# Another order for VectorE's operations inside each step of a graph-attention kernel's edge loop

## The reference, cut to what matters

```python
kj = k[src] + e                     # e = edge features @ We
alpha = sum(q[dst] * kj, axis=-1) / sqrt(C)
m = segment_max(alpha, dst)
a = exp(alpha - m[dst])
s = segment_sum(a, dst)
vj = v[src] + e
out = segment_sum((a / s[dst])[..., None] * vj, dst)
```

## Time and profile before

| what | value |
|---|---|
| median of the runs | 7153.44 us |
| the profiled execution, its own time | 7176.55 us |
| its span, first to last instruction | 7174.9 us |
| POOL busy | 5053.5 us, 70% |
| VectorE busy | 4453.4 us, 62% |
| TensorE busy | 4422.2 us, 62% |
| ScalarE busy | 997.8 us, 14% |
| moved over the span | 94 GB/s on average |

### The profile page before, as it was taken

One profiled execution on the slowest core, in us unless ns is written; L12 is line 12 of the kernel. 1 busy time (PEld: TensorE's weight loads), 2 busy tenths in 40 slices (PEclk: granted clock), 3 DMA queues, 4 the chain that ended last, 5 costly groups with the idle time before them and its releaser, 6 DMA issues. The chain is left out here.

```text
span 7174.9 us, 154717 instructions
## 1 busy us (share of the span) xinstructions
PE 4422.2 (62%) x36620; PEld 3475.0 (48%) x36620; DVE 4453.4 (62%) x15728; ACT 997.8 (14%) x4122; POOL 5053.5 (70%) x5118
## 2 busy tenths in 40 slices
PE   7996555555555556665656565566555555555555
PEld 5775444444444445444444444445444444444444
DVE  6556666666666666666666666666666666666666
ACT  2222111111111112111111111112111111111110
POOL 2225777777777775777777777775777777777775
PEclk8995555555555555555555555555555555555555
DMA  4553333333333333333333333333333333333332
GB/s 121 159 154 95 89 90 91 90 90 90 90 91 91 90 90 88 93 92 91 92 90 94 91 92 91 92 93 89 92 89 89 90 90 90 90 91 90 90 89 71
DMA packets 687687, 675.84 MB, mean 94 GB/s; under 512 B 369234, under 2 KB 506388, under 8 KB 687636
## 3 DMA queue, kind: packets, MB, share of 16 engines
q0 software_dynamic: 161600, 320.52, 18.2%
q1 hardware_dynamic: 496944, 301.76, 15.7%
q10 hardware_dynamic: 29092, 52.97, 2.5%
HBM read 652.96 MB, written 21.67 MB: 94 GB/s over the span
## 5 line engine op out<-in xcount | busy, mean ns | idle before, releaser
L1355 POOL DMA_INDIRECT Gall<-KV,sdn x4848 | 4905.9, 1012 | 1515.8 <-issue 950.6
L752 DVE TENSOR_TENSOR kj<-Gall,pE 128x512 f32<-128x512 f32 x606 | 417.0, 688 | 2225.1 <-DMA Gall<-KV,sdn 2222.5
L932 PE MATMUL pY<-fw,Ob 128*42 128x6 bf16 (+1 forms) x4848 | 257.8, 176 | 1735.0 <-DVE cr L805 1734.8
L946 PE MATMUL pG<-O,vals 128*66 128x42 f32 (+1 forms) x10784 | 1296.6, 308 | 0.7 <-ACTq L988 0.7
L946 PEld LDWEIGHTS pG<-O,vals 128*66 128x66 f32 (+1 forms) x10784 | 1205.8, 223 | 47.5 <-ACT vals L982 28.8
L932 PEld LDWEIGHTS pY<-fw,Ob 128*42 128x42 bf16 x4848 | 222.7, 121 | 1789.7 <-issue 1789.4
L959 ACT ACTIVATE fw<-lm 128x16 bf16<-128x16 f32 (+1 forms) x606 | 135.8, 224 | 5374.2 <-DVE O L720 5374.2
L879 PE MATMUL pE<-bd,ea 128*128 128x256 f32 x1212 | 739.6, 714 | 13.5 <-PEq L988 13.5
L884 PE MATMUL pE<-bd,ea 128*128 128x256 f32 x1212 | 642.4, 633 | 0.0
L939 PEld LDWEIGHTS pM<-Mb,OTs 42*128 42x128 bf16 x4848 | 178.2, 101 | 937.6 <-issue 937.6
L939 PE MATMUL pM<-Mb,OTs 42*128 42x6 bf16 (+1 forms) x4848 | 212.2, 163 | 528.7 <-DVE df L823 520.2
(11 more groups left out here) (185 smaller groups left out, 6082.2 us busy)
## 6 DMA issues: line engine op xcount, KB each, us to landing
db<-D SPq DMA_DIRECT2D x606, 256.0 KB
ea<-in_ea SPq DMA_DIRECT2D x606, 128.0 KB
Gall<-KV,sdn POOLq DMA_INDIRECT x4848
db<-D ACTq DMA_DIRECT2D x202, 256.0 KB, 3.6
qw<-QT SPq DMA_DIRECT2D x1818, 5.2 KB
dr<-in_dr SPq DMA_DIRECT2D x1212, 4.0 KB
ea<-in_ea SPq DMA_DIRECT2D x202, 64.0 KB, 3.5
sdn<-in_sdn SPq DMA_DIRECT2D x606, 12.0 KB
```

Of the source, the lines that this page charges most:

```text
L752: return e.tensor_tensor(kj[:, :, :], G[u][:, :, 0:64], pE[u][:, :].rearrange("p (j c) -> p j c", c=64), ALU.add)
L932: return e.matmul(pmn[:, j, :], lhs, rhs, start=False, stop=j == T)
L946: return e.matmul(sums[u][0:AR, 0:W], vals[u][:, j, 0:AR], O[u][:, j, :], start=j == 0, stop=j == T - 1)
L1355: e.indirect_dma_start(G[u][:, j, :], None, kvtab, bass.IndirectOffsetOnAxis(ap=sdn[u][:, j:j + 1], axis=0)).then_inc(s_g[u], 16)
```

## The change

VectorE's operations of a step get another order. OT moves from behind df to behind cr. facc and acc leave the place between O and X. vals moves from the end of the step to right behind df, facc and acc follow it, and the scan is last. TensorE's wait ahead of its fac product names VectorE's acc of the block before instead of vals of the same block. The other engines' programs, the gates of the gathers and the operations themselves stay as they are.

```diff
@@ order of VectorE's operations in a step
-                "V": ["A kj", "A vj", "B fhi", "B fm", "B flo", "B cr", "A prod", "A alpha", "C d1", "C d", "Z cont",
-                      "Z last", "A flag", "A O", "D facc", "D acc", "B X", "B Mhi", "B Mm", "B Mlo", "B df", "Z OT",
-                      "A scan", "C vals"],
+                "V": ["A kj", "A vj", "B fhi", "B fm", "B flo", "B cr", "Z OT", "A prod", "A alpha", "C d1", "C d",
+                      "Z cont", "Z last", "A flag", "A O", "B X", "B Mhi", "B Mm", "B Mlo", "B df", "C vals",
+                      "D facc", "D acc", "A scan"],
@@ vector_step: v_OT
                 missing(e, "V", t, "fhi", "cr")
+            if "Z" in on:
+                v_OT(e, zt).then_inc(pV, 1)
+            else:
+                missing(e, "V", t, "OT", "OT")
             if "A" in on:
@@ vector_step: v_facc, v_acc leave the place between v_O and v_X
-            if "D" in on:
-                if "A" not in on:
-                    after(e, "P", "agg7", dt)
-                if "C" not in on:
-                    after(e, "V", "acc", dt - 1)
-                v_facc(e, dt).then_inc(pV, 1)
-                v_acc(e, dt).then_inc(pV, 1)
-            else:
-                missing(e, "V", t, "facc", "acc")
@@ vector_step, behind v_df
-            if "Z" in on:
-                v_OT(e, zt).then_inc(pV, 1)
-            else:
-                missing(e, "V", t, "OT", "OT")
+            if "C" in on:
+                v_vals(e, ct).then_inc(pV, 1)
+            else:
+                missing(e, "V", t, "vals", "vals")
+            if "D" in on:
+                if "A" not in on:
+                    after(e, "P", "agg7", dt)
+                if "C" not in on:
+                    after(e, "V", "acc", dt - 1)
+                v_facc(e, dt).then_inc(pV, 1)
+                v_acc(e, dt).then_inc(pV, 1)
+            else:
+                missing(e, "V", t, "facc", "acc")
             if "A" in on:
                 v_scan(e, at).then_inc(pV, 1)
             else:
                 missing(e, "V", t, "scan", "scan")
-            if "C" in on:
-                v_vals(e, ct).then_inc(pV, 1)
-            else:
-                missing(e, "V", t, "vals", "vals")
@@ tensor_step
             if "D" in on:
-                after(e, "V", "vals", dt)
+                after(e, "V", "acc", dt - 1)
                 hold(e)
                 p_fac(e, dt)
```

## The result

The changed kernel takes **6999.33 us** (median of 4 runs, 6992.85 to 7009.77); the kernel before took 7155.15 (4 runs, 7152.58 to 7170.39) beside it. The ratio is 0.9782, 95% interval 0.9765 to 0.9798: 2.2% faster. The forecast was 7150 us, no change, with a range of 7060 to 7270. The time lies outside it. The profiled execution took 6998.85 us, with a span of 6997.2.

What follows compares the result with a forecast made beforehand. POOL's gathers, stopped by vals, and a loop through O and SP's loads were taken as the bounds. 603 steps x (10.48 - 10.487) = -4 us gave 7172 profiled, hence 7150 us, no change; range 7060 to 7270.

Steps and rivals of the forecast that it cites:

- first loop: POOL's gathers with vals in their way: floor 9.99 us a step, with 0.50 us a step lying above it.
- second: Loop of kj, O, SP's loads, the last gather's landing and the next kj, with its own floor, 10.06 us.
- step B: Second-pass step of the profile before, 10.06 us: seventh gather not stopped by vals, next kj 4.43 us after db's issue.
- I count nothing: Whether a gather holds up VectorE's operations: no cost forecast; the shared-port rule would have added 0.10 us a step.
- the price of O's delay: O and the loads waiting for it come 0.40 us later, putting the next kj at 10.34 to 10.68, taken as 10.46.
- the load loop: O + 1.86 to db's issue, then 4.43 to next kj; claimed to set the step, leaving POOL's possible gain unused.
- B's 4.43: Time in us from db's issue to the next kj in step B, used to price every changed step.
- POOL then must lose: POOL's gathers lose 0.49 us a step: 0.23 at O and vals, the remaining 0.26 at the gather OTs stops.
- The forecast's place of the row: OTs, O and vals each stop a gather; the last one starts 7.28 us after kj, 1.25 behind db.
- Rival 1: Loads don't bind, only blocking of gathers counts: kj 2.63 after the last gather, about 10.0 a step, 6860 us; chance 0.14.
- Rival 2: Later loads make it slower: kj 4.65 behind db, step 10.68 us, +116 us, 7270 us; chance 0.17.
- Rival 3: Gathers aren't freed: vals, held up by w, still stops one for 0.73 us; +70 to +98 us, 7235; chance 0.08.

Runs made afterwards that it cites:

- ot_acc_early: Kernel before with OTs behind cr, facc and acc behind df, vals still last, and ea and db issued behind prod instead of O: 6868.45 us.
- rest_only_3: Changed kernel with OTs put back between acc and the scan, the rest of the change kept: 0.9662 of the kernel before.
- after_early_3: Changed kernel with SP's big loads ea and db issued behind VectorE's prod instead of behind O: 6904.97 us.
- acc_only: Kernel before with facc and acc alone moved from behind O to behind df, vals still last: the whole gain; its time is not in the text.
- vals_only: Kernel before with vals alone moved from the step's end to right behind df: the whole gain; its time is not in the text.
- ot_early: Kernel before with OTs behind cr and ea and db issued behind prod; facc and acc stay behind O, vals last: 7133.54 us.

## Why the prediction was wrong

- *What bounds the kernel* was read rightly in its first loop, POOL's stopped gathers, and wrongly in its second: the landing behind the loads holds kj up in many steps, but never POOL, whose gathers go on 0.30 us apart. The first loop's size was right too: the gathers lost 0.54 us a step before ((1012 - 944) x 8) and 0.16 after, and with 0.02 lost (ot_acc_early) a step takes 9.97, which is the floor of 9.99.
- *Times of VectorE's operations* were right: medians of 1.71 for OTs, 4.20 for O, 5.51 for vals. vals takes 0.69, not 0.65, in its new place, which was not foreseen. The slide of the scan was hidden as forecast: TensorE's wait for it grew from 332 to 732 us, its wait for cr fell from 1735 to 1150.
- *The Trainium skill (SBUF — State Buffer, section "Who interferes with whom")*, by which an operation with two SBUF inputs contends with POOL's reads and the first holds the shared ports, would have made O stand until a gather had ended. No O does: in the first step above O starts 0.25 us into a gather and takes 0.55, and none of the changed kernel's takes over 0.58. The trace disagrees with that reading, as step B did. "I count nothing" was wrong for OTs alone, which can take up to 0.7 (last section), 0.50 on the mean.
- **The failed step** is the price of O's delay, and with it that "the load loop, 0.40 us longer, sets the step": next kj "with B's 4.43" at 10.46, for every step. 4.43 behind db holds while the last gather starts 1.1 to 1.5 behind db. I had three steps with that spacing and made a floor of it. It changes with that distance: 3.84 to 3.90 under 0.5 us. rest_only_3, where O is not delayed, gives the method's own number (O + 1.86 + 4.43 = 10.06; measured 10.09, 10.13, 10.08). That is no proof of the loop, and may be luck: POOL's account gives its middle steps too, 9.99 + 0.10 lost + 0.06 in pauses = 10.15. OTs' delay then brought the forecast to 10.48; measured, it added 10.19 - 10.10 = 0.09: some 0.06 in stopped gathers and 0.04 in pauses of POOL. Against the profiled execution the miss is 7172 - 6999 = 173 us, and 603 x (10.48 - 10.194) = 172.
- *The gathers' places* were linked to the failed step. I let OTs stop a gather in each step, since "POOL then must lose" the difference to a fixed 10.48, 0.49 us a step. It lost 0.16 (a mean gather of 964 ns, not 1005) and paused 0.09. It loses nearly nothing when the row of requests runs one place ahead: OTs, O and vals start 1.7, 4.2 and 5.5 behind kj, 2.5 and 1.3 apart, about two spacings and one, so a row that passes one of them should pass them all (argued from the spacings, not tested). The forecast's place of the row and the one 1.25 us ahead of it both repeat themselves; the prediction took the first for all steps.
- *Rival 1* (6860, 0.14) had the side but not the mechanism: kj follows the last gather by 3.50 (median), not by 2.63. Taking the loads away as well makes it true (6905, 6868). *Rival 2*: in the group that was forecast kj stands 4.46 behind db on the mean, not 4.65. *Rival 3*: no gathers of 1.67 us are left, the longest takes 1.54.
- *The range* ended at 7060 because the landing was priced from one spacing, 4.31 to 4.65, and nothing below it; the steps at 3.85 were outside it.

For the change as a whole: the gain comes from vals leaving the start of the seventh gather (its cost fell from 280 to 43 us). Not all of that is distance: in 84 steps of the changed kernel vals still starts up to 0.2 us behind a gather's start, and the gather takes 0.94; what protects it there is open. Of its parts, vals behind df or facc and acc behind df are each enough, and OTs' move works against them (0.9662 without, 0.9782 with it) as long as the loads wait for O. The Trainium skill (DMA: Bandwidth & Descriptors, section "Issuing engines are not separate DMA queues") puts the loads and the gathers in the same engines; the traces agree, as kj's distance to the last gather falls to 2.65 once the loads are moved away (after_early_3).

## What to carry to other kernels

When one engine's requests come at a fixed pace and another's operations can stop them, look at the difference of their starts, over all steps and not in three; a stop vanishes when the operation moves by 0.3 us one way (acc_only) or 0.9 the other (vals_only), and what is changed far off (when the loads are issued) moves the whole row onto or off it. A latency that was read at one spacing is no floor at another, and a loop that holds up one engine doesn't set the pace while the busiest one never waits for it. Take a change apart before keeping it: here one part of it cost a third of what the other gave (1.2 of 3.4%), and became worth something only once a third thing, the loads, was moved.

## What the runs showed of the hardware

- A gather whose start lies from 0.2 us ahead of vals to some 0.1 before vals' end completes 0.82 us after vals ends, where vals stands behind the scan (median of over 1000; up to 0.74 us lost). The front edge depends on what stands ahead of vals: behind df, in the four kernels with the changed order, the 346 gathers that start up to 0.2 ahead of it take 0.94 to 0.96 us like any other. There vals itself takes 0.69 instead of 0.65. Neither was looked into.
- A gather doesn't hold up O or vals, whose times don't depend on where in a gather they start, but it holds up OTs: of those in the attention passes of the kernel before, the 130 that start 0.5 to 0.6 us behind a gather's start take 0.65 us on the mean, where those that start 0.7 to 1.0 behind it take 0.48.
- In the changed kernel POOL pauses before the second gather of every thirteenth block (every 104 gathers), and goes on about when the gathers that were under way have landed: 45 pauses in the middle steps, 55 us above the usual 0.30, and two of 0.66 us in the kernel before. The timeline after:

```profile
1413.62 0.69 DVE L752 TENSOR_TENSOR kj<-Gall,pE 128x512 f32<-128x512 f32 x1 [3.07 <-DMA Gall<-KV,sdn]
1413.87 0.94 POOL L1355 DMA_INDIRECT Gall<-KV,sdn  x1 [1.74 <-issue]
```

  By the table of gates this gather waits for the scan of two blocks before, which had ended at 1410.55, so that isn't it. ot_early has no such pause and ot_acc_early five of 0.53 us, but after_early_3, whose gathers stand as close to kj as in ot_acc_early, has 45 of 0.69. What POOL waits for is not shown.
- Chips differ by more than any edit here: 22% in the kernel before, and with the opposite sign of the change (1.0108 against 0.9782). Signals of TensorE come late there; that this is the whole difference is not shown, as the kernel before has no trace from such a chip.
